# First block of a mixture-of-experts stage: order on TensorE, and who splits the expert weights

## The reference

```
shared = relu(xt @ sW1 + sb1) @ sW2 + sb2
probs  = softmax(xt @ router_W + router_b)
cw     = the 3 largest of 15 probabilities, zero elsewhere
h      = relu(xt @ eW1[e] + eb1[e])                    for 15 experts
routed = sum over e of cw[:, e] * (h @ eW2[e] + eb2[e])
x      = x + shared + routed
```

## Time and profile before

| what | us |
|---|---|
| median of 3 runs (lowest to highest) | 2231.68 (2230.51 to 2232.52) |
| the profiled execution | 2236.0 |
| its span, first to last instruction | 2234.3 |
| TensorE busy | 1862.4 (83%) |
| VectorE busy | 1685.1 (75%) |
| ScalarE busy | 1203.0 (54%) |
| GpSimd busy | 914.2 (41%) |

### The profile page before, as it was taken

One profiled execution on the slowest core, in us unless ns is written; L12 is line 12 of the kernel. 1 busy time (PEld: TensorE's weight loads), 2 busy tenths in 40 slices (PEclk: granted clock), 3 DMA queues, 4 the chain that ended last, 5 costly groups with the idle time before them and its releaser, 6 DMA issues. The chain is left out here.

```text
span 2234.3 us, 31060 instructions
## 1 busy us (share of the span) xinstructions
PE 1862.4 (83%) x9650; PEld 1280.5 (57%) x9650; DVE 1685.1 (75%) x4185; ACT 1203.0 (54%) x2004; POOL 914.2 (41%) x887
## 2 busy tenths in 40 slices
PE   6886499998699967673499978999999999967998
PEld 4554377776577723332377755555555555536777
DVE  6997688876588879998588867766767767636886
ACT  3442266652466634442366654666665655545666
POOL 1110355542355522220355544534543544234555
PEclk8998699999799998876699989999999999978999
DMA  3000344420444410000244410000000000004444
GB/s 99 6 5 4 110 158 143 143 72 1 143 143 143 143 39 1 1 0 0 72 146 160 156 39 1 1 1 1 1 1 1 1 1 1 1 1 143 162 167 138
DMA packets 87704, 142.28 MB, mean 64 GB/s; under 512 B 12369, under 2 KB 24337, under 8 KB 87026
## 3 DMA queue, kind: packets, MB, share of 16 engines
q1 hardware_dynamic: 85232, 139.50, 18.7%
q10 hardware_dynamic: 2306, 0.78, 0.2%
HBM read 136.38 MB, written 3.87 MB: 63 GB/s over the span
## 5 line engine op out<-in xcount | busy, mean ns | idle before, releaser
L2336 ACT ACTIVATE soft_prob<-psum 128x1024 f32<-128x1024 f32 (+3 forms) x384 | 302.4, 812 | 203.9 <-PE psum L2216 202.2
L2428 DVE TENSOR_REDUCE soft_mx<-psum 128x1 f32<-128x512 f32 (+2 forms) x352 | 230.8, 687 | 116.4 <-PE psum L2286 79.5
L2286 PE MATMUL psum<-soft_own,soft_stack 128*128 128x512 f32 (+3 forms) x768 | 249.4, 377 | 24.4 <-DVE soft_mx L2424 10.5
L2216 PE MATMUL psum<-soft_stack,soft_own 128*128 128x512 f32 (+3 forms) x768 | 225.5, 377 | 2.8 <-POOL soft_stack L2193 2.2
L2424 DVE CUSTOM_DVE_ANT_0 psum<-psum,s_soft_sel 128x384 f32<-128x384 f32 (+1 forms) x256 | 157.2, 638 | 65.0 <-PE psum L2286 64.4
L2216 PEld LDWEIGHTS psum<-soft_stack,soft_own 128*128 128x128 f32 x768 | 125.2, 189 | 133.1 <-issue 80.8
L2286 PEld LDWEIGHTS psum<-soft_own,soft_stack 128*128 128x128 f32 x768 | 139.8, 193 | 92.6 <-DVE soft_mx L2428 43.0
L2199 POOL TENSOR_SCALAR_AFFINE_SELECT soft_prob<-soft_prob 128x256 f32<-128x256 f32 x256 | 102.5, 407 | 203.9 <-ACT soft_prob L2336 201.0
L163 POOL TENSOR_TENSOR norm_rstd<-norm_mv,s_const_minus_half 128x4 f32<-128x4 f32 x64 | 65.1, 1018 | 279.3 <-DVE norm_mv L158 273.2
L2233 PE MATMUL psum<-soft_prob,soft_v_pad 128*32 128x512 f32 (+3 forms) x1536 | 163.7, 498 | 3.5 <-ACT soft_prob L2336 2.1
L940 POOL TENSOR_TENSOR ffn1b_low<-ffn1b_full,ffn1b_high 128x512 fp32r<-128x512 f32 x80 | 103.0, 1293 | 105.0 <-ACT ffn1b_high L1083 82.5
(11 more groups left out here) (440 smaller groups left out, 4977.7 us busy)
## 6 DMA issues: line engine op xcount, KB each, us to landing
ffn0a_cwb<-ffn0a_cw_dram SPq DMA_DIRECT2D x120, 256.0 KB, 6.2
ffn0b_cwb<-ffn0b_cw_dram SPq DMA_DIRECT2D x120, 256.0 KB, 6.4
ffn1a_cwb<-ffn1a_cw_dram SPq DMA_DIRECT2D x120, 256.0 KB, 6.3
ffn1b_cwb<-ffn1b_cw_dram SPq DMA_DIRECT2D x120, 256.0 KB, 6.1
s_ffn_w<-in_ffn_w SPq DMA_DIRECT2D x4, 1024.0 KB, 8.0
out_x<-x SPq DMA_DIRECT2D x8, 256.0 KB, 7.4
x<-in_x SPq DMA_DIRECT2D x4, 384.0 KB, 7.5
mamba_coef_dram<-mamba_out_coef SPq DMA_DIRECT2D x8, 96.0 KB, 1.6
```

The lines of the kernel that those rows point to most:

```text
L2216: ins = pe.matmul(e_ps[:, n % 2, j, low(n):BLK], own[:, u % 3, 2 * pair + j, kt * P:(kt + 1) * P], stack[:, u % HT, qb * BLK + low(n):(qb ...
L2286: ins = pe.matmul(per_head[:, n, :], stack[:, u % HT, i * P:(i + 1) * P], own[:, u % 3, g, half * BLK:half * BLK + width], start=(n == 0), ...
L2336: nc.scalar.activation(prob[:, done % PROBS, :, low(n):BLK], e_ps[:, n % 2, :, low(n):BLK], ACT.Exp, scale=float(HD) ** -0.5).then_inc(exp ...
L2428: nc.vector.tensor_reduce(mx[:, i, half, heads.start:heads.stop], bank[:, 0:width * len(heads)].rearrange("p (g k) -> p g k", k=width), AX ...
```

## The change

- TensorE, first block: `transpose_cw(0)`, then `tokens(1)` and `route(1)`, all behind `up(3)`; it no longer waits for `cw_one`. `route(q)` waits for `cwt_ready` in place of `cwx_ready`.
- ScalarE: `copy_x(1)` directly behind `copy_cwt(0)`; in every block `cwx` is copied ahead of `cwt`.
- GpSimd: one piece (w1, experts 0 to 3), then a wait for `cw_ready`, then w1 of experts 4 to 7, `norm.invert(1)`, and w2 of experts 0 to 3 and 4 to 7.
- VectorE: the low parts of experts 8 to 15 of w1 and w2, behind `norm.scale(1)` and ahead of `weigh(0)`. `up(8)` and `down(8)` wait for them.

```diff
--- before.py
+++ after.py
@@ -876,6 +876,7 @@
         xt_high, xt_split, stored = sem("xt_high"), sem("xt_split"), sem("stored")
         piece_loaded = [sem(f"piece_loaded{i}") for i in range(PIECES_KEPT)]
         W_PIECES = (0, 4, 8, NE)
+        w1_low_rest, w2_low_rest = sem("w1_low_rest"), sem("w2_low_rest")
         more_blocks = BLOCKS + (out is None)
 
         block = ctx.enter_context(nc.Block())
@@ -928,7 +929,7 @@
 
             def low_weights(which, i):
                 some = slice(W_PIECES[i], W_PIECES[i + 1])
-                pool.wait_ge(w_high, 1 if which == 0 and i == 0 else 2 if which == 0 else 3)
+                pool.wait_ge(w_high, (1 if i == 0 else 2) if which == 0 else 3)
                 dst, src, done = ((w1_parts, w["w1"], w1_ready), (w2_parts, w["w2"], w2_ready))[which]
                 nc.gpsimd.tensor_tensor(dst[1][:, some, :], src[:, some, :], dst[0][:, some, :], ALU.subtract)\
                     .then_inc(done, 1)
@@ -942,9 +943,13 @@
 
             split_x(0)
             if split:
-                for which, i in ((0, 0), (0, 1), (1, 0), (0, 2), (1, 1), (1, 2)):
-                    low_weights(which, i)
+                low_weights(0, 0)
+                pool.wait_ge(cw_ready, 1)
+                low_weights(0, 1)
             norm.invert(pool, 1)
+            if split:
+                low_weights(1, 0)
+                low_weights(1, 1)
             for g in range(BLOCKS):
                 for e in range(NE):
                     if e not in ON_VECTOR:
@@ -962,7 +967,7 @@
                 pe.wait_ge(norm.xt_ready, q + 1)
                 pe.wait_ge(logit_used, q)
                 if q:
-                    pe.wait_ge(cwx_ready, q)
+                    pe.wait_ge(cwt_ready, q)
                 for j in range(GT):
                     ins = pe.matmul(logit_ps[:, j, 0:E], norm.xt[:, q % 2, j * P:(j + 1) * P], w["router"][:, :],
                                     start=True, stop=True)
@@ -983,8 +988,10 @@
                         pe.wait_ge(high_ready, m + 1)
                     else:
                         pe.wait_ge(scaled_ready, routed_up_to(m))
-                if split and g == 0 and e in W_PIECES:
+                if split and g == 0 and e in W_PIECES[:2]:
                     pe.wait_ge(w1_ready, W_PIECES.index(e) + 1)
+                if split and g == 0 and e == W_PIECES[2]:
+                    pe.wait_ge(w1_low_rest, 1)
                 if e == 0:
                     pe.wait_ge(xt_high, g + 1)
                 for i, (part, xpart) in enumerate(((0, 0), (1, 0), (0, 1))):
@@ -1003,8 +1010,10 @@
                     if g >= 2:
                         pe.wait_ge(y_copied, g - 1)
                     pe.matmul(y_ps[:, g % 2, :], b2_parts[:, :], cwt[:, g % 2, :], start=True, stop=False)
-                if split and g == 0 and e in W_PIECES:
+                if split and g == 0 and e in W_PIECES[:2]:
                     pe.wait_ge(w2_ready, W_PIECES.index(e) + 1)
+                if split and g == 0 and e == W_PIECES[2]:
+                    pe.wait_ge(w2_low_rest, 1)
                 pe.wait_ge(high_ready, n + 1)
                 slot = n % HIGH_RING
                 pe.matmul(y_ps[:, g % 2, :], w2_parts[0][:, e, :], high[:, slot, :], start=False, stop=False)
@@ -1028,18 +1037,19 @@
                     ins = pe.transpose(back_ps[:, j, :], yt[:, j * P:(j + 1) * P], const["ident"][:, :])
                 ins.then_inc(back_ready, 1)
 
-            pe.wait_ge(cw_one, 1)
             route(0)
             for n in range(EXPERTS):
                 g, e = divmod(n, NE)
                 up(n)
                 if n == H_BANKS - 1:
                     transpose_cw(0)
+                    tokens(1)
+                    route(1)
                 if n >= LAG:
                     down(n - LAG)
-                if e == 0 and g + 1 < more_blocks:
+                if e == 0 and 0 < g and g + 1 < more_blocks:
                     tokens(g + 1)
-                if e == 3 and g + 1 < BLOCKS:
+                if e == 3 and 0 < g and g + 1 < BLOCKS:
                     route(g + 1)
                 if e == 6 and g:
                     back(g - 1)
@@ -1086,10 +1096,10 @@
                 act.wait_ge(cwt_ps_ready, q + 1)
                 if q >= 2:
                     act.wait_ge(down_done, NE * (q - 2) + 1)
-                nc.scalar.copy(cwt[:, q % 2, :], cwt_ps[0:B2_ROWS, :, :]).then_inc(cwt_ready, 1)
                 if q:
                     act.wait_ge(stored, 16 * q)
                 nc.scalar.copy(cwx[EXACT:EXACT + NE, :], cwt_ps[EXACT:EXACT + NE, :, :]).then_inc(cwx_ready, 1)
+                nc.scalar.copy(cwt[:, q % 2, :], cwt_ps[0:B2_ROWS, :, :]).then_inc(cwt_ready, 1)
 
             def copy_y(g):
                 act.wait_ge(down_done, NE * (g + 1))
@@ -1107,10 +1117,11 @@
                 nc.scalar.copy(w2_parts[0][:, :, :], w["w2"][:, :, :]).then_inc(w_high, 1)
                 nc.scalar.copy(b2_parts[:, :], w["b2"][:, :]).then_inc(b2_high, 1)
             copy_cwt(0)
+            copy_x(1)
             for n in range(EXPERTS):
                 g, e = divmod(n, NE)
                 parts_of(n)
-                if e == 1 and g + 1 < more_blocks:
+                if e == 1 and 0 < g and g + 1 < more_blocks:
                     copy_x(g + 1)
                 if e == 4 and g + 1 < BLOCKS:
                     exp(g + 1)
@@ -1196,6 +1207,11 @@
                 xg = x[:, g * GT:(g + 1) * GT, :]
                 nc.vector.tensor_tensor(xg, back_ps[:, :, :], xg, ALU.add).then_inc(x_added, 1)
 
+            def low_weights(dst, src, done):
+                some = slice(W_PIECES[2], NE)
+                nc.vector.tensor_tensor(dst[1][:, some, :], src[:, some, :], dst[0][:, some, :], ALU.subtract)\
+                    .then_inc(done, 1)
+
             norm.resume(dve)
             nc.vector.memset(prob[:, :, E:E + 8 - TOPK], -1.0)
             nc.vector.memset(cw[:, :, E:NE], 1.0)
@@ -1211,6 +1227,10 @@
                                         ALU.subtract).then_inc(b2_ready, 1)
             norm.statistics(dve, 1)
             norm.scale(dve, 1)
+            if split:
+                dve.wait_ge(w_high, 3)
+                low_weights(w1_parts, w["w1"], w1_low_rest)
+                low_weights(w2_parts, w["w2"], w2_low_rest)
             for n in range(EXPERTS):
                 g, e = divmod(n, NE)
                 if e < E:
```

## The result

The changed kernel takes 2178.74 us (median of 4 runs, 2175.81 to 2182.36), the kernel before 2231.35 us (2230.51 to 2232.52) beside it: ratio 0.9765, 95% interval 0.9748 to 0.9782, 52.6 us less. It is faster, 13.0 us above the forecast of 2165.7 and inside its range. Its profiled execution took 2175.81 us (span 2174.1 us, mean clock 0.939), against 2236.0 us (span 2234.3 us, clock 0.926) before: 60.2 us less.

What follows compares the result with a forecast made beforehand. TensorE was taken to bound the mixture bodies, with waiting in the heads ahead of them. Head gains of 18.8 + 18.2 + 16.5 + 13.4 = 66.9 us, taken as 66, off the median 2231.68 gave 2165.7, range 2153 to 2186.

Steps and rivals of the forecast that it cites:

- The heads: Four mixture stages, routing to the fifth `up` group, up(4): mostly waiting; gains 18.8, 18.2, 16.5 and 13.4 us, sum 66.9.
- Rival 3: VectorE's stretched small instructions weren't GpSimd's doing: `cw` stays 7.2 us late in three stages, 16 us less gained, 2182; 3%.
- Scaling behind both pieces: ffn1b: VectorE's scaling of the next tokens held behind GpSimd's two w2 pieces, 1.27 us each, ending at 2001.8.
- The choice between the bounds: End of that scaling in ffn1b: lower bound 1999.6, upper 2003.1; 2001.8 taken.
- The two splits: VectorE, behind the scaling: two 128x1024 splits, 2.44 us together; 5.0 with one GpSimd piece in front of each.
- The token path: ffn1b: next tokens' transposes, copies and logits end last before up(4), 1 us behind `scaled`.
- rival 2: VectorE becomes last of the head, held by GpSimd: 3.8 us more in three stages, 8 us less gained, 2174; 14%.
- its length doesn't depend on what went before it: The body, up(4) to the last transposes back, is TensorE's and keeps its 205 us after the change.
- No later wait is added: Behind up(4): experts 8 to 15 are split by 2004.3, first used four `up` groups later; no cost.
- rival 1: Pipeline behind up(4) isn't primed: three missing experts at ScalarE's 1.2 us, 3.6 us a stage back, 2179; 13%.
- the 2 us of "sooner": Clock: with a shorter pause, the 2.4 GHz level may come sooner, up to 2 us a stage gained.
- the 1.5 of "later": Clock: in a broken start, the 2.4 GHz level may come later, 1.5 us lost.

Runs made afterwards that it cites:

- order_only: Against the changed kernel: TensorE's and ScalarE's new order kept, all low parts back on GpSimd, none on VectorE; 2188.81 us, 0.9783 of the kernel before.
- scale_first: Against the changed kernel: GpSimd's two w2 pieces wait for the scaling of the next tokens; 2181.51 us, 0.9753 of the kernel before.
- fetch_later: Against the changed kernel: in ffn0a, the next layers' weights load behind the second block's broadcasts; 2171.95 us, 0.9720 of the kernel before.
- primed: Against the changed kernel: the first block's up(4) waits for four `scaled` tiles instead of one; 2178.89 us, 0.9756 of the kernel before.
- again: The changed kernel unaltered, run and profiled once more; 2177.95 us, 0.9736 of the kernel before.
- late_cw: Against the changed kernel: block 1's weights' transposes and their copies two experts later, first block only; 2180.97 us, 0.9744 of the kernel before.
- early_cw: Against the changed kernel: VectorE's and ScalarE's routing of block 1 two experts sooner; 2177.07 us, 0.9739 of the kernel before.

## Why the prediction was right, and by how much it missed

**The heads** were right, each within 1 us: ffn1b 19.4 for 18.8 forecast, ffn1a 18.9 for 18.2, ffn0a 15.8 for 16.5, ffn0b 14.0 for 13.4; 68.1 for 66.9.

- The small VectorE instructions from L1173 to L1179 are at 0.2 us in all stages, and order_only brings the copies back at 2.27, 1.30 and 2.26. Rival 3 is out. Of L1135's wait, though, the forecast left "some hundredths"; L1146 still takes 0.78 to 0.85 us in the splitting stages, 0.6 more than unhindered.
- Scaling behind both pieces: forecast end 9.8 us behind L1135 (1992.04 to 2001.8), measured 1949.79 to 1959.86, 10.1 us. The choice between the bounds was right, and scale_first shows the reason.
- The two splits: 2.44 us forecast from the form of another line, 2.35 measured, each 1.21 and in no stage held. The token path ended last in ffn1a and ffn1b, as I had it; rival 2 is out.
- up(4) 14.1 us behind L1146 in ffn1b, forecast 14.1.
- ffn0a: store landed by 256.7 in the forecast, first broadcast issued at 256.68; up(4) 261.2 forecast, 261.10 measured, behind `scaled`. Part of this is luck: the stage began 0.8 us sooner than before, so that the head came out 0.7 us longer than forecast. fetch_later shows that the fetch costs this head 4 us.
- ffn0b: up(4) released by `scaled` (0.79 us), as forecast.

**The step that failed** is the first one: "its length doesn't depend on what went before it", said of the body, and with it "No later wait is added" and "bodies still 205 us". Down(0) did follow; the transposes of block 1's weights, behind expert 8, met a wait that grew by 7.1 us over the four stages, and the bodies are 9.4 us longer. The sum counted the heads alone and put this term at nothing. The mechanism is rival 1's, which stood at 13%: the pipeline isn't primed. Its sign, a body longer than 206 us, came in three of four stages. Its size was off: it had 3.6 us a stage, and it is 2.3 on average (9.4 / 4). I had charged it to ScalarE; the wait is for VectorE. How much of it is VectorE's `scaled`, how much its instructions stretched beside GpSimd, no run takes apart. My argument against the rival, that TensorE needs 2.56 us an expert at 1.2 GHz, holds only for the 3 to 6 us until the clock rises, and beyond that VectorE has its routing of block 1 to do as well. primed shows the mechanism by removal and return.

**The clock.** Behind up(4) the low level lasted 4.6, 4.6, 4.0 and 5.0 us before, and 3.8, 2.9, 5.8 and 4.2 in the changed kernel. Halved, three stages gained 0.4 to 0.8 us and ffn1a lost 0.9, so neither the 2 us of "sooner" nor the 1.5 of "later" came; in `again` ffn0b had 6.3 us for 2.9. The 2.4 GHz level came during the `up` groups, but TensorE waits again before up(4), whose first matmul takes 0.77 to 0.80 us, as before. What the forecast didn't have is the second low stretch of 3.4 us behind the new wait, in one stage of the changed kernel and in all four of scale_first.

**From the execution to the median.** The forecast took 66 off both. By the profiled executions it was 60.2: 2.1 more than forecast in the heads, 9.4 lost in the bodies, 1.5 gained elsewhere. That is 5.8 of the miss. The execution of before lay 4.65 us above its median of 2231.35, that of after 2.93 below its own: 7.6 more. With the 0.3 us by which before's median moved, 5.8 + 7.6 - 0.3 = 13.1, the distance of 13.0. Over half of the miss is thus which executions were profiled. That the remainder is as small as 5.8 is in part luck: the failed term alone is worth 9.4.

## What to carry to other kernels

A pause in front of a busy stretch is also the time in which the other engines build a lead. Before counting its removal in full, count what each of them will have finished at the new start, and look for the first instruction of the bottleneck that needs the one that is then behind: here 68 us of pause gave 60. When such a wait is moved and the time stays, don't conclude yet that it is work on an engine and not order. Sum up the bottleneck's idle time and its granted clock: in late_cw the idle time stayed, in early_cw most of it went and the low clock took the gain.

## What the runs showed of the hardware

- VectorE and GpSimd hold each other, and in the pairs seen here the hold falls on whichever comes second: VectorE's 128x64 copy took 2.27 us for 0.19 behind a GpSimd piece; GpSimd's two pieces took 4.55 us for 2.48 beside VectorE's two 128x1024 splits, which took 2.36 either way. The Trainium skill (GPSIMD Engine Reference, Key points) names the collision for VectorE instructions with two SBUF inputs or in a two-port mode; the trace agrees for the splits, and which mode the copy runs in no row shows.
- VectorE's 128x128 moments beside a GpSimd piece aren't held: four took 0.87 us from 1954.20, while a piece ran from 1953.94 for 1.39; before, from 2003.11 with no piece running, they took 0.87 too.
- Behind a wait of TensorE of 1.8 to 3.8 us the clock fell for 3.4 us in some stages and not in others (of the changed kernel's four waits only behind the 3.77; in scale_first behind all, 2.06 among them), each time costing 1.7 us. In late_cw and early_cw it fell so in five stages behind a wait of only 1.1 us, at L972. What decides it stays open. Body = 201.5 to 203.1 us + the wait at the transposes + half the time at the low level fits all stages in which those transposes stand where the changed kernel has them and block 1's routing too.
